# Summing conv taps in PSUM, gating z beside the next image's first chunk, and reading that chunk from SBUF

## The reference

```
xz = in_proj_w @ gn(x);  xx, z = split(xz)              # 192 + 192 channels
xx = gelu(depthwise_conv3x3(xx) + conv_b)
4 scan directions over the 2304 pixels (rows, columns, and both backwards):
    dts, B, C = x_proj_w[k] @ xx;  delta = softplus(dt_w[k] @ dts + dt_b[k])
    h = h * exp(delta * A) + delta * xx * B;   y_k = sum over states of h * C  + Ds[k] * xx
y = layernorm over channels(sum of y_k) * ln_w + ln_b;   x1 = x + out_proj_w @ (y * gelu(z))
qkv = depthwise_conv3x3(w_qkv @ gn(x1));  q, k normalised per head (8 heads of 12)
out = x1 + w_proj @ (softmax(q k^T * scale) v)
```

## Time and profile before

| what | value |
| --- | --- |
| median of the timed runs | 10277.98 us |
| lowest and highest of 3 | 10254.69 and 10307.78 us |
| profiled execution | 10287.01 us |
| its span, first to last instruction | 10285.2 us |
| TensorE's granted clock over the span | 0.825 |
| busy in the span: PE, DVE | 7907.0, 7526.2 us |
| busy in the span: ACT, POOL | 6467.1, 6297.6 us |
| DMA traffic | 1537.26 MB |

### The profile page before, as it was taken

One profiled execution on the slowest core, in us unless ns is written; L12 is line 12 of the kernel. 1 busy time (PEld: TensorE's weight loads), 2 busy tenths in 40 slices (PEclk: granted clock), 3 DMA queues, 4 the chain that ended last, 5 costly groups with the idle time before them and its releaser, 6 DMA issues.

```text
span 10285.2 us, 176575 instructions
## 1 busy us (share of the span) xinstructions
PE 7907.0 (77%) x54832; PEld 2574.0 (25%) x54832; DVE 7526.2 (73%) x6480; ACT 6467.1 (63%) x11834; POOL 6297.6 (61%) x4443
## 2 busy tenths in 40 slices
PE   5576668887788877888788886888878874888658
PEld 2122222222222222222222222222222221222212
DVE  1688758886788867887588867888578876889630
ACT  2343348774577746776477755777467763877468
POOL 0577637774587746776377745777368773777320
PEclk7565579988898988888798988889889885999789
DMA  2556525654356525665156543555255551565200
GB/s 62 161 178 197 179 68 186 192 181 122 126 187 188 185 71 181 190 187 176 63 186 189 187 127 122 182 187 186 77 169 188 181 182 51 187 192 178 86 26 20
DMA packets 768722, 1537.26 MB, mean 149 GB/s; under 512 B 85528, under 2 KB 412996, under 8 KB 758800
## 3 DMA queue, kind: packets, MB, share of 16 engines
q1 hardware_dynamic: 767760, 1525.52, 47.5%
HBM read 1272.74 MB, written 252.44 MB: 148 GB/s over the span
## 4 chain that ended last, share of the span: by engine, by line
PE 37%; issue 18%; DVE 14%; DMA 11%; ACT 10%; POOL 5%; SPq 4%; ACTq 0%; DVEq 0%; POOLq 0%
PE ps L1842 7%; PE ps L1774 6%; DMA job_u<-u_scratch 6%; PE ps L1762 5%; PE ps L1710 4%; ACT probs_buf L1226 4%; DVE rings L1440 4%; DVE ps L1419 3%; DVE job_buf L1440 3%; PE ps L1749 2%; POOL hc_buf L993 2%; PE ps L1942 1%; PE ps L1943 1%; PE ps L1791 1%; ACT rings L1213 1%
## 5 line engine op out<-in xcount | busy, mean ns | idle before, releaser
L1226 ACT ACTIVATE probs_buf<-ps 128x384 f32<-128x384 f32 x6912 | 3146.4, 491 | 1197.9 <-PE ps L1842 1131.1
L993 POOL TENSOR_TENSOR hc_buf<-rings,rep 128x768 f32<-128x768 f32 x1152 | 2091.4, 1815 | 1207.1 <-DVE rings L1440 793.6
L1842 PE MATMUL ps<-qp_buf,kp_buf 108*128 108x384 bf16 x6912 | 2289.8, 352 | 605.0 <-ACT probs_buf L1226 274.4
L993 POOL TENSOR_TENSOR hc_buf<-job_buf,rep 128x768 f32<-128x768 f32 x1152 | 2092.0, 1816 | 994.2 <-DVE job_buf L1440 989.0
L1419 DVE TENSOR_TENSOR ps<-ps,rep 128x768 f32<-128x768 f32 x2304 | 2177.3, 945 | 525.4 <-PE ps L1750 420.2
L1774 PE MATMUL ps<-probs_buf,v_buf 128*13 128x384 f32 x13824 | 1584.7, 533 | 77.7 <-DVE att_buf L1458 46.6
L1762 PE MATMUL ps<-hc_buf,sum_states 128*32 128x144 f32 x24576 | 1508.1, 333 | 144.0 <-POOL hc_buf L993 110.3
L1749 PE MATMUL ps<-st_buf,pick_channel 96*128 96x512 bf16 x2304 | 1011.3, 439 | 601.4 <-DVE rings L1440 232.4
L1440 DVE TENSOR_TENSOR_SCAN job_buf<-rings,ps 128x768 f32<-128x768 f32 x768 | 1368.7, 1782 | 101.1 <-ACT rings L1213 54.8
L1842 PEld LDWEIGHTS ps<-qp_buf,kp_buf 108*128 108x128 bf16 x6912 | 649.7, 98 | 3090.4 <-ACT probs_buf L1226 2132.9
L1213 ACT ACTIVATE st_buf<-st_buf,a_cols 128x768 f32<-128x768 f32 x1152 | 1062.0, 927 | 92.1 <-DMA st_buf<-delta_scratch 91.5
(11 more groups left out here) (190 smaller groups left out, 8297.3 us busy)
## 6 DMA issues: line engine op xcount, KB each, us to landing
st_buf<-delta_scratch SPq DMA_DIRECT2D x1152, 384.0 KB
rings<-delta_scratch SPq DMA_DIRECT2D x1152, 384.0 KB
part_scratch<-job_buf SPq DMA_DIRECT2D x1152, 72.0 KB, 3.3
st_buf<-part_scratch SPq DMA_DIRECT2D x192, 432.0 KB, 7.0
rep<-xd_scratch SPq DMA_DIRECT2D x192, 384.0 KB
job_u<-u_scratch SPq DMA_DIRECT2D x192, 192.0 KB
delta_scratch<-job_buf SPq DMA_DIRECT2D x192, 192.0 KB, 4.8
qp_buf<-qk_scratch SPq DMA_DIRECT2D x864, 36.0 KB
```

The costliest lines, as they stand in the source:

```text
L993: pool.tensor_tensor(hc[tile % 2][:, chunk(kk, v)], h_ring[t % 2], rep_third(1, kk, v), ALU.mult).then_inc(s["hc_ready"], 1)
L1226: act.activation(probs[(m % 2) * HG + h], bank(slots["score", p]), ACT.Exp, scale=SCALE)\
L1842: pe.matmul(bank(slots["score", p]), k_parts[:, h, m * 128:(m + 1) * 128], q_ring[:, (kk * NS + q) % 2, h, :], start=True, stop=True).then ...
```

## The change

It has six parts, and they touch the backs and the first front only.

- `conv` sums its taps in three banks of PSUM. Each tensor is done in two halves of 24 rows, nine passes each; a pass reads the window from SBUF and the sum from PSUM, the ninth writes to SBUF. Every pass waits for the one before, through `chain.link`.
- The gates of z (`gates`, on PE and ACT) run beside the front's chunk 0, between its gelus and the table load behind them, in banks 5 and 7, one chunk at a time; `zg` now holds all six.
- Only chunk 0 of the front stands ahead of y (`AHEAD = 1`); chunk 1 joins chunks 2 to 5 beside the conv, and `FRONT_UNITS` and `FRONT_SUMS` are moved to fit.
- Chunks 0 and 1 are read from `xs` in SBUF; the first load from DRAM is chunk 2's, issued behind the loads of y and u.
- DVE adds the two squared parts, so the variance takes one matmul for each chunk. The scaling by 1/std takes ln_w with it, and ln_b goes with the multiplication by z: two passes instead of three.
- Of the last 16 y stores of a scan, ACT issues 8.

The front inside the first scan stays as it was.

```
-FRONT_UNITS = tuple((3 + 3 * (c - 2) + i, c, part) for c in range(2, NPC) for i, part in enumerate(("gelu", "out")))
-FRONT_SUMS = (4, 7, 10, 13)
+AHEAD = 1
+FRONT_UNITS = tuple((2 + 3 * (c - AHEAD) + i, c, part) for c in range(AHEAD, NPC) for i, part in enumerate(("gelu", "out")))
+FRONT_SUMS = (3, 6, 9, 12, 15)
...
-        zg = [[rep[:, (2 * i + t) * PC:(2 * i + t + 1) * PC] for t in range(2)] for i in range(2)]
+        zg = [probs_buf[:, 0:6 * PC], rep[:, 13 * PC:16 * PC]]
...
@@ SP: directions, back
-                        store_y(kk, NS - 1, 0, 16)
+                        store_y(kk, NS - 1, 0, 8 if kk + 1 == K else 16)
...
                 sp.wait_ge(s["y_stored"], (b + 1) * (2 * NS * 256))
                 apart(sp)
-                if fb is not None:
-                    first_chunk(fb)
                 sp.dma_start(y[0], y_dram[0, 0:DA, :]).then_inc(s["y_loaded"], 16)
...
+                if fb is not None:
+                    first_chunk(fb)
                 if not (isinstance(b, int) and b == 0):
                     store_out(b - 1)
@@ POOL: transpose of chunk 0
+                            if not inside_scan(fb):
+                                pool.wait_ge(s["f_in"], 2 * (n + 2))
@@ ACT: front_part, directions, back
                     act.activation(uc[0][:, :], bank(2), ACT.Gelu, bias=conv_bias[0][:, :])\
                         .then_inc(s["f_gelu"], 1)
+                    if between is not None:
+                        between()
                     act.preload_act_table_set(LN_EXP_TABLES)
...
+                act.wait_ge(s["y_ev"], (b + 1) * K * NT)
+                apart(act)
+                for j in range(8, 16):
+                    rows8 = y_dram[1, 8 * 2 * TG * (NS - 1):8 * 2 * TG * NS, j * YP:(j + 1) * YP]
+                    src = y_acc[8 * j:8 * j + 8, 2 * TG * YP * (NS - 1):2 * TG * YP * NS]
+                    act.dma_start(rows8.rearrange("(t d) r -> d t r", d=8),
+                                  src.rearrange("p (t r) -> p t r", r=YP)).then_inc(s["y_stored"], 16)
                 last_leftover(ab, fb)
...
+                def gates():
+                    for c in range(NPC):
+                        act.wait_ge(s["z_mm"], b * NPC + c + 1)
+                        part, cols = rows(c)
+                        act.activation(zg[0][:, piece(c)], bank(5), ACT.Gelu)
+                        act.activation(zg[1][part, cols], ps[part, 7, 0:PC], ACT.Gelu).then_inc(s["z_act"], 1)
                 if fb is not None:
-                    first_chunks(fb, 2)
+                    front_pads(fb, 0)
+                    front_part(fb, 0, "gelu", gates)
+                    front_part(fb, 0, "out")
+                else:
+                    gates()
+                    act.preload_act_table_set(LN_EXP_TABLES)
@@ DVE: conv, back
+                acc = ps[0:C, 5:8, 0:PC].rearrange("p a (h w) -> p a h w", w=W)
+                for j, (dst, pad, w) in enumerate(work):
+                    for hf in range(2):
+                        half_rows = slice(hf * (H // 2), (hf + 1) * (H // 2))
+                        for tap in range(9):
+                            src = window(pad, tap)[:, half_rows, :].rearrange("p (a h) w -> p a h w", a=3)
+                            to = acc if tap < 8 else \
+                                square(dst)[:, half_rows, :].rearrange("p (a h) w -> p a h w", a=3)
+                            if tap == 0:
+                                ins = dve.tensor_scalar(to, src, w[:, 0:1], None, ALU.mult)
+                            else:
+                                ins = dve.scalar_tensor_tensor(out=to, in0=src, scalar=w[:, tap:tap + 1], in1=acc,
+                                                               op0=ALU.mult, op1=ALU.add)
+                            if (j, hf, tap) == (len(work) - 1, 1, 8):
+                                ins.then_inc(s[done], 1)
+                            else:
+                                chain.link(ins)
...
+                    if c:
+                        part, _ = rows(c - 1)
+                        whole, rest = (x[part, :] for x in sq[(c - 1) % 2])
+                        dve.wait_ge(s["ln_sq"], b * NPC + c)
+                        dve.tensor_tensor(whole, whole, rest, ALU.add).then_inc(s["ln_sqf"], 1)
...
                     for t, p, x in both(c):
-                        ins = dve.tensor_tensor(x, x, rstd[p, piece(c)], ALU.mult)
+                        ins = dve.scalar_tensor_tensor(out=x, in0=x, scalar=ln_w[t][p, :], in1=rstd[p, piece(c)],
+                                                       op0=ALU.mult, op1=ALU.mult)
                     chain.link(ins)
-                        ins = dve.tensor_scalar(x, x, ln_w[t][p, :], ln_b[t][p, :], ALU.mult, ALU.add)
-                        ins = dve.tensor_tensor(x, x, zg[c % 2][t][p, :], ALU.mult)
+                    for (t, p, x), z in zip(both(c), (zg[0][:, piece(c)], zg[1][part, cols])):
+                        ins = dve.scalar_tensor_tensor(out=x, in0=x, scalar=ln_b[t][p, :], in1=z,
+                                                       op0=ALU.add, op1=ALU.mult)
@@ PE: front_in, front_chunk, back
+                top = W if c == 0 else 0
+                rows10 = xc[:, :] if c >= 2 else xs[:, (8 * c - 1) * W + top:(8 * c + 9) * W]
...
                 if c + 1 < CHUNKS:
                     front_in(fb, c + 1)
+                if between is not None:
+                    between()
...
+                def gates():
+                    pe.wait_ge(s["xn_loaded"], 16 * (b + 1))
+                    for c in range(NPC):
+                        if c:
+                            pe.wait_ge(s["z_act"], b * NPC + c)
+                        part, _ = rows(c)
+                        pe.matmul(bank(5), in_proj[:, DI:DI + DA], xn[:, piece(c)], start=True, stop=True)
+                        pe.matmul(ps[part, 7, 0:PC], in_proj[:, DI + DA:2 * DI], xn[:, piece(c)],
+                                  start=True, stop=True).then_inc(s["z_mm"], 1)
...
-                    first_chunks(fb, 2)
-                    pe.wait_ge(s["f_pad"], 2 * (fb * CHUNKS + 3))
+                    front_in(fb, 0)
+                    front_chunk(fb, 0, gates)
+                    pe.wait_ge(s["f_pad"], 2 * (fb * CHUNKS + AHEAD + 1))
+                    pe.wait_ge(s["f_xd"], fb * 12 + AHEAD)
...
-                        over_channels(bank(2 + j), (mean192[:, :], mean192), (sq[j][0], sq[j][1][part, :]), c - 1)\
-                            .then_inc(s["ln_var"], 1)
+                        pe.matmul(bank(2 + j), mean192[:, :], sq[j][0], start=True, stop=True)\
+                          .then_inc(s["ln_var"], 1)
...
                     pe.wait_ge(s["qkv_ev"], (b + 1) * NPC)
-                    for c in range(2, CHUNKS):
+                    for c in range(AHEAD, CHUNKS):
                         front_chunk(fb, c)
                 for n in range(NORMS):
                     pe.wait_ge(s["n_sq"], b * NORMS + n + 1)
+                    if fb is not None and n == 1:
+                        pe.wait_ge(s["f_xd"], fb * 12 + 6)
```

More of the change, by code:

```diff
@@ L47 @@
 LN_EXP_TABLES = "natural_log_exp_and_others"
-DVE_CHAIN = 35
+DVE_CHAIN = 47
 PIECES = MB * HG
@@ L1142, in front_pads, with front_part @@
                         apart(act)
[L1143 to L1146 removed]
+                    top = 1 if c == 0 else 0
+                    dst = pads[i][:, :].rearrange("p (h w) -> p h w", w=PADW)[:, top:, 1:1 + W]
+                    act.copy(dst, square(ps[0:p, i, top * W:XC])).then_inc(s["f_pad"], 1)
+            def front_part(fb, c, part, between=None):
                 n = fb * CHUNKS + c
```

127 lines of the change are left out of this document (55 added, 72 removed).

## The result

The changed kernel takes 10100.56 us, median of 4 runs (10092.42 to 10107.39), against 10276.24 (10254.69 to 10307.78, 4 runs) beside it: ratio 0.9829, 95% interval 0.981 to 0.9848. It is 176 us faster; the prediction said 10087, so it came out 13.6 us above the number and inside the range.

What follows compares the result with a forecast made beforehand. Bound: eight backs of some 280 us with no engine busy throughout. Five loop backs −69, first back −9.4, two without a front −104.8, start −7: together −190, profiled 10097, median 10087; rivals A to D span 9967 to 10238.

Steps and rivals of the forecast that it cites:

- the tails: Stretch from the conv's end to the next scan: claimed to stay as it was, nothing lost.
- Part 1: Six backs with a front: earlier chunk 0 and gates start the mean 18.8 us earlier in the second back.
- cover: Load path of y in a back: y summed by 2475, 12 us before the mean wants it.
- Part 2: Norm with one variance matmul pair fewer per chunk, at half clock: 30.7 us against 22.8, +7.9 in the second back.
- Part 3: Scaling and out-projection, two DVE passes per chunk and z ready: 21.3 us instead of 36.1, −14.8 in the second back.
- Part 4: Conv, 36 half-length passes not held by POOL: 53 us on DVE, −25.6 without a front, +9.6 with one.
- Part 5: Small ones: first front starts 7 us earlier; the two backs without a front gain 52.4 us each.
- Rival A: TensorE's clock stays full through gates and norm: 20 us less per back with a front, 9967; chance 0.24.
- B: POOL and DVE still take turns in the conv: 94 us without a front, 101 with, 10238; chance 0.07.
- C: ACT's store issues cost 3.61 us each: all eight backs lose 26 us, 10295, slower than before; chance 0.04.
- D: Smaller gain: conv taps 2.0 us rather than 1.47, gates and x_proj later by 8 in six backs, about 10155; chance 0.10.

Runs made afterwards that it cites:

- experiment 6: Changed kernel with two pairs of PSUM banks for the gates instead of one: 10068.54 us, ratio 0.9792.
- 3: Changed kernel, but TensorE starts chunk 0 only when the store of xn has landed in DRAM: 10161.72 us, ratio 0.9881.
- 2: Changed kernel with all six z gates moved back, between the norm and the scaling: 10273.9 us, ratio 0.9987.
- Experiment 5: Two runs on the changed kernel: variance by two matmuls without VectorE's add, 10131.37 us; third bank for the mean and variance two chunks behind, 10050.01 us.
- experiment 4: Changed kernel with all 16 of y's last stores issued by SP again: 10095.04 us, ratio 0.9818.
- kernel 8: Changed kernel with two gate bank pairs, deeper norm (third bank, variance two chunks behind), all stores on SP and needless matmuls in TensorE's waits: 9906.39 us, ratio 0.9628.

## Why the prediction was right, and where not

- **The sum.** That the total came out within 14 us owes something to luck. The norms are 26 us dearer than forecast over eight backs, the start and the tails 24 us cheaper, and neither was foreseen.
- **Part 1, the mean.** Right: −115 against −108 in six backs, and the releaser is the front's chain. Two errors pulled opposite ways. ScalarE's issues cost 0.46 to 0.60 each and not 0.36, and chunk 0 started 9.5 us after T0 in the second back, not 7.5; but the six gates took 19.4 us there and not 23.7, for two or three of them ran at full clock and not one. That the load had cover was right (8.6 us of it in the second back, where I had 12; experiment 6 uses it up), and so were the serial chain (3) and that the gates' place carries the gain (2).
- **Part 2, the norm.** The clock was right (half), the pace wrong: "three pairs of 1.58 are 4.74 a chunk". I named the chain mean, subtract, square, add, variance, but priced it only at full clock, at 2.9 us a chunk, where it measures 4.20 (2467.34 to 2471.54); at half clock its 6.1 to 6.2 us are above TensorE's 4.74. The step that failed is thus the one that says the subtraction queued behind the add costs only at full clock. Measured +10.7 a back instead of +7.9, and without a front −3.1 and −5.3 instead of −8.7. Experiment 5 shows the loop: with a third bank and one more chunk of distance the wait is gone.
- **Part 3.** Right: 21.6 against 21.3, a pitch of 3.05, −73 against −75. This is read from the trace; no run of the changed kernel has the three passes back, so what the merged passes and what the ready z give isn't separated.
- **Part 4.** Right in both kinds of back: 52.3 against 53 and 96.2 to 97.0 against 96. That VectorE's passes with one operand in PSUM and POOL's sums don't hold each other up was an inference from the scan's rows; 112 passes within 3 ns of each other and POOL's 128 sums between 2602 and 2644 show it. The page "SBUF — State Buffer" of the Trainium skill (Who interferes with whom) states the same: an instruction of VectorE with at most one input in SBUF, outside what the page calls its two-port modes, doesn't contend with GpSimd, and one with two inputs in SBUF contends with a GpSimd instruction that reads SBUF. The runs agree on both sides, 1.42 without spread here, 2.6 to 8.0 with the sums in SBUF.
- **Part 5.** Backs without a front: −47 each against −52, the difference being the norm's. The start: −15.7 against −7. The kernel before has its first T0 at 1229.5; with only the conv changed it is 1219.9, and the kernels that have the new start lie between 1211.5 and 1221.9, so a single profile doesn't resolve the 8.7. The tails' −14.8 are of the same kind: they lie between 43 and 55 us before the change and between 43 and 50 after it, and no experiment gave them a cause.
- **Rival A** was half of the truth: the clock didn't stay full, but it does so for the most part when TensorE's waits are filled, and then 77 to 92 us come back. Its 20 us a back were too much for the changed kernel (11 measured), since in the norm the loop's waits remain and take a chunk to 4.20 us even at full clock. **Rivals B and C** fell: no turns in the conv, issues of 0.60 us at most, far from 3.35; of D neither part came, with passes of 1.42 and a mean 3 us earlier than forecast in the second back. D's price was also short: 19 us in each of two backs and 8 in six give 10173, not 10155. And three chunks between 2599.60 and 2650.41 are 16.94 apiece and not 16.84, the last having waited; neither slip moved the forecast.

## What to carry to other kernels

When an add moves from TensorE to another engine, price the loop that it closes (product, handover, subtraction, add, handover, next product) at the clock that the stretch will have, not the busiest engine alone; one more chunk of distance, here with a third bank, opens it. Where TensorE hands single products to and fro, its own waits cost twice, once as waits and once as the lower clock behind them: more banks first, and needless matmuls in what remains. And ask of a contended pair who waits for the slower one: here VectorE's turns with POOL cost ScalarE 1.8 to 3.8 us a back, off the engine pair itself, and only until another chunk covered it.

## What the runs showed of the hardware

- TensorE stayed at 1.2 GHz through 36 us in which it was busy for 34.6 without a wait (experiment 5, eight times alike), yet went back to 2.4 GHz inside the deeper norm, whose products stand back to back too (2442.85 to 2460.88), and even for one chunk in the changed kernel's norm, where it waits 1.57 us or more per chunk (2467.34). The page "TensorE: Matmul & The Clock Gate" of the Trainium skill (Part 1: The HAM clock gate) says that sustained activity releases the gate. By that rule the 36 us would have ended at full clock; the trace doesn't agree there, and what tells these stretches apart stays open.
- DMA issues take longer when two engines issue at once: 16 on SP alone took 5.69 to 6.07 us in the kernel before (0.36 to 0.38 apiece), 8 on each of SP and ScalarE 3.65 to 4.22 us (0.46 to 0.53) in seven backs of the changed kernel and 4.86 (0.60) in one. Both have outliers (6.85 for 16 in one back of experiment 4), so one back doesn't give the price.
- Within one execution of kernel 8 the same norm took 15.7 us in six backs and 22.3 and 22.6 in two: which level of the clock a back meets isn't set by the program alone.
